# First layer's ffn: the elementwise steps of gate, up half and products dealt out anew over VectorE, ScalarE and GpSimd

## What is computed

```python
def act_qdq(x):
    qmax = 2.0 ** (ACT_BITS - 1) - 1.0
    scale = jnp.maximum(jnp.max(jnp.abs(x)) / qmax, 1e-12)
    return jnp.clip(jnp.round(x / scale), -qmax - 1.0, qmax) * scale

def fixed_qdq_u16(x):
    scale = 1.0 / 65536.0
    return jnp.clip(jnp.round(x / scale), 0.0, 65535.0) * scale
...
x = act_qdq(x)
up = act_qdq(x @ lpbq_dequant(w_up).T)
gate = act_qdq(x @ lpbq_dequant(w_gate).T)
sig = fixed_qdq_u16(jax.nn.sigmoid(gate))
gate = act_qdq(gate * sig)
o = act_qdq(gate * up)
return o @ lpbq_dequant(w_down).T
```

## Time and profile before

| | |
|---|---|
| median of three runs | 1481.43 us (1481.37 to 1482.19) |
| time of the profiled execution | 1482.96 us |
| its span, first to last instruction | 1481.1 us |
| TensorE busy | 1277.1 us (86%) |
| VectorE busy | 848.2 us (57%) |
| ScalarE busy | 697.4 us (47%) |
| GpSimd busy | 269.6 us (18%) |
| mean granted TensorE clock | 0.949 of full speed |

### The profile page before, as it was taken

How to read it: one execution, slowest core, us unless ns; L and a number is a source line. 1 busy time by engine, 2 the same in 40 slices (tenths; PEclk the granted TensorE clock), 3 DMA queues, 4 the chain that set the end, 5 groups by cost and what they waited for, 6 DMA issues and landing times.

```text
span 1481.1 us, 26043 instructions
## 1 busy us (share of the span) xinstructions
PE 1277.1 (86%) x9173; PEld 952.2 (64%) x9173; DVE 848.2 (57%) x1776; ACT 697.4 (47%) x1361; POOL 269.6 (18%) x454
## 2 busy tenths in 40 slices
PE   4799860879988879998888989979999998898989
PEld 2465520446667769876666868668778754456877
DVE  4888679544444456646666443456564466665242
ACT  1566678445533424434444434333433366565453
POOL 1899201000002122331000003042330021100000
PEclk9899975889998979999999999989999999999999
DMA  8000100402220113103404000113101000000000
GB/s 296 1 2 2 47 26 0 191 1 115 101 92 16 51 31 95 56 26 115 182 1 192 1 4 24 43 48 105 42 22 75 1 2 1 1 2 1 1 15 15
DMA packets 42605, 75.69 MB, mean 51 GB/s; under 512 B 3816, under 2 KB 33520, under 8 KB 41584
## 3 DMA queue, kind: packets, MB, share of 16 engines
q1 hardware_dynamic: 38384, 65.62, 12.1%
q0 software_dynamic: 4096, 8.40, 1.9%
HBM read 59.72 MB, written 14.29 MB: 50 GB/s over the span
## 4 chain that ended last, share of the span: by engine, by line
PE 70%; DVE 14%; ACT 8%; issue 5%; POOL 2%; DVEq 1%; DMA 1%; ACTq 0%; SPq 0%; POOLq 0%
PE bank L1576 7%; PE bank L1565 7%; PE bank L1561 6%; PE bank L1620 5%; PE bank L1546 4%; PE bank L1629 4%; PE bank L1547 3%; PE bank L1552 3%; PE bank L1358 3%; PE bank L1424 3%; PE bank L1363 2%; PE bank L1365 2%; PE bank L1364 2%; PE bank L1474 2%; PE bank L1440 1%
## 5 line engine op out<-in xcount | busy, mean ns | idle before, releaser
L1801 ACT ACTIVATE SC<-bank 128x512 f32<-128x512 f32 x192 | 114.3, 596 | 253.6 <-PE bank L1546 133.9
L1888 DVE SCALAR_TENSOR_TENSOR SC<-bank,SM,SC 128x512 f32<-128x512 f32 x128 | 95.9, 749 | 148.0 <-PE bank L1565 108.7
L2458 POOL DMA_INDIRECT xs<-CC,POSI x64 | 62.7, 980 | 564.1 <-DVE POSI L2264 474.6
L1565 PE MATMUL bank<-X,SC 128*128 128x128 f32 x1024 | 140.1, 281 | 14.6 <-DVE SC L2150 14.5
L1576 PE MATMUL bank<-A,SC 128*128 x1024 | 137.0, 277 | 9.0 <-DVE SC L1888 8.3
L1561 PE MATMUL bank<-X,SC 128*128 128x128 f32 x1024 | 140.2, 281 | 5.3 <-ACT SC L1796 5.3
L1561 PEld LDWEIGHTS bank<-X,SC 128*128 128x128 f32 x1024 | 130.9, 198 | 19.5 <-issue 13.6
L1565 PEld LDWEIGHTS bank<-X,SC 128*128 128x128 f32 x1024 | 128.2, 197 | 16.5 <-DVE SC L2150 16.3
L1576 PEld LDWEIGHTS bank<-A,SC 128*128 128x128 f32 x1024 | 126.2, 193 | 18.8 <-issue 18.8
L1620 PE MATMUL bank<-A 128*128 128x128 f32 x736 | 103.5, 286 | 11.5 <-DVE A L2283 10.2
L1712 ACT ACTIVATE A<-bank,SM 128x128 f32<-128x128 f32 x256 | 73.8, 384 | 65.9 <-DVE SM L1984 65.5
(11 more groups left out here) (308 smaller groups left out, 2485.6 us busy)
## 6 DMA issues: line engine op xcount, KB each, us to landing
A<-in_moe SPq DMA_DIRECT2D x36, 768.0 KB, 11.9
A<-xs SPq DMA_DIRECT2D x20, 256.0 KB, 4.3
ys<-A SPq DMA_DIRECT2D x20, 256.0 KB, 2.4
BW<-in_l1f SPq DMA_DIRECT2D x2, 2048.0 KB, 10.4
BW<-in_l2f SPq DMA_DIRECT2D x1, 3456.0 KB, 11.1
BW<-in_l1c SPq DMA_DIRECT2D x1, 3072.0 KB, 16.7
BW<-in_l3f SPq DMA_DIRECT2D x1, 2816.0 KB, 9.6
A<-in_l1c SPq DMA_DIRECT2D x1, 2560.0 KB, 8.5
```

Source lines behind the costliest of these rows:

```text
L1565: m = e.matmul(at["pu"].ap[:, cut(q)], wx[:, cut(4 + q)], x, start=True, stop=True)
L1801: e.activation(at["h"].ap, at["pg"].ap, ACT.Gelu_apprx_tanh).then_inc(at["gelu"][0], 1)
L1888: return e.scalar_tensor_tensor(out=o, in0=a, scalar=s, in1=b, op0=o1, op1=o2)
```

## The change

It deals out steps in another way; the arithmetic of each result stays the same.

- g1 goes from VectorE to GpSimd (`tensor_scalar`) for all twelve items.
- g3 goes from VectorE to ScalarE for the items (0,2) and (1,2), there as two instructions with the constants `P192` and `N192`; the product g4 of these items then cuts off with a minimum.
- `upq` is put into the gate stage's rounds, behind g2 of the same item. For (1,1), (2,1) and (3,1) its first step stays on ScalarE; for the other nine it goes to GpSimd. Its second step is on GpSimd for all twelve. Nothing stands between the reduce and the small steps of the scale any more.
- Products: for m = 0 the second step of p0 and the product go to GpSimd, as a `tensor_scalar` and a `tensor_tensor`; for m = 1 and 2 the product is one `stt` on VectorE.
- `dq`: for m = 0 the second step goes to GpSimd.

Cut to the changed lines and some of what stands around them:

```diff
-        MAG, NMAG = sm(1), sm(1)
+        MAG, NMAG, P192, N192 = sm(1), sm(1), sm(1), sm(1)
...
         def gate_item(n, m):
-            u = {}
+            u, on = {}, "act" if m == 2 and n < 2 else "dve"
...
             def f1():
...
-                at["t"] = u["t"] = tick("f0_vec")
+                at["t"] = u["t"] = tick("f0_ppool")
...
             def f2():
...
+                up_step(n, m)
...
             def f3():
-                at = step("g3", s=u["s"], prev=u["t"])
-                at["t"] = u["t"] = tick("f0_vec")
+                at = step("g3", s=u["s"], prev=u["t"], on=on)
+                if on == "act":
+                    at["grid"] = tick("f0_act")
+                at["t"] = u["t"] = tick("f0_act" if on == "act" else "f0_vec")
...
             def f4():
-                at = step("g4", G=G, s=u["s"], prev=u["t"])
+                at = step("g4", G=G, s=u["s"], prev=u["t"], on=on)
...
         def up_step(n, m):
...
-            at = step("upq", Uq=Uq, ui=ui, us=us, ready=tu_)
-            at["act"], at["t"] = tick("f0_act"), tick("f0_vec")
-            tu[n, m] = at["t"]
+            at = step("upq", Uq=Uq, ui=ui, us=us, ready=tu_, on="act" if m == 1 and n else "pool")
+            at["q"] = tick("f0_act" if at["on"] == "act" else "f0_ppool")
+            at["t"] = tu[n, m] = tick("f0_ppool")
...
         in_order([gate_item(n, m) for n, m in nms], done)
-        g2s, g2i, t2 = scale_of(mg2, 12, sig["g2"], lambda: [up_step(*nm) for nm in nms[:8]])
-        for nm in nms[8:]:
-            up_step(*nm)
+        g2s, g2i, t2 = scale_of(mg2, 12, sig["g2"])
...
         def prod_item(n, m):
-            u = {}
+            u, pooled = {}, m == 0
...
             def f0():
-                at = step("p0", G=G, g2i=g2i, ready=t2)
-                at["q"], at["t"] = tick("f0_act"), tick("f0_act")
-                u["t"] = at["t"]
+                at = step("p0", G=G, g2i=g2i, ready=t2, pooled=pooled)
+                at["q"] = u["t"] = tick("f0_act")
+                if not pooled:
+                    at["t"] = u["t"] = tick("f0_act")
...
             def f1():
-                pooled = m == 1 and n < 3
...
-                at["t"] = u["t"] = tick("f0_vec")
...
-                    at["tp"] = u["t"] = tick("f0_ppool")
+                    at["s"] = tick("f0_ppool")
+                at["t"] = u["t"] = tick("f0_ppool" if pooled else "f0_vec")
...
             def f3():
...
             def s0():
...
-                    at = step("dq", G=gu(n, m)[0], osc=osc, oiv=oiv, on="dve" if m == 2 else "act", ready=t3)
+                    at = step("dq", m=m, G=gu(n, m)[0], osc=osc, oiv=oiv, on="dve" if m == 2 else "act", ready=t3)
...
-                    at["t"] = u[m] = tick("f0_vec")
+                    at["t"] = u[m] = tick("f0_ppool" if m == 0 else "f0_vec")
...
             def s1():
...
                     w.wait_ge(*at["prev"])
...
-                elif kind == "upq":
-                    w.wait_ge(*at["ready"])
-                    e.activation(at["Uq"], at["Uq"], ACT.Identity, scale=at["ui"], bias=MAG).then_inc(at["act"][0], 1)
+                elif kind == "g3" and at["on"] == "act":
+                    w.wait_ge(*at["prev"])
+                    e.activation(at["s"].ap, at["s"].ap, ACT.Identity, bias=P192).then_inc(at["grid"][0], 1)
+                    w.wait_ge(*at["grid"])
+                    e.activation(at["s"].ap, at["s"].ap, ACT.Identity, bias=N192).then_inc(at["t"][0], 1)
+                elif kind == "upq" and at["on"] == "act":
+                    w.wait_ge(*at["ready"])
+                    e.activation(at["Uq"], at["Uq"], ACT.Identity, scale=at["ui"], bias=MAG).then_inc(at["q"][0], 1)
                 elif kind == "p0":
...
                     e.activation(at["G"], at["G"], ACT.Identity, scale=at["g2i"], bias=MAG).then_inc(at["q"][0], 1)
-                    w.wait_ge(*at["q"])
-                    e.activation(at["G"], at["G"], ACT.Identity, bias=NMAG).then_inc(at["t"][0], 1)
+                    if not at["pooled"]:
+                        w.wait_ge(*at["q"])
+                        e.activation(at["G"], at["G"], ACT.Identity, bias=NMAG).then_inc(at["t"][0], 1)
                 elif kind == "dq" and at["on"] == "act":
...
+                    e.memset(P192, 192.0)
+                    e.memset(N192, -192.0)
...
                 elif kind == "f0_ymax":
...
-                elif kind == "g1":
-                    w.wait_ge(*at["prev"])
-                    w.wait_ge(*at["ready"])
-                    ts(at["G"], at["G"], MAGIC, at["gs"], ALU.subtract, ALU.mult).then_inc(at["t"][0], 1)
-                elif kind == "g3":
+                elif kind == "g3" and at["on"] == "dve":
                     w.wait_ge(*at["prev"])
...
                 elif kind == "g4":
                     w.wait_ge(*at["prev"])
-                    stt(at["G"], v4(at["s"].ap), 192.0, at["G"], ALU.subtract, ALU.mult).then_inc(at["t"][0], 1)
+                    if at["on"] == "dve":
+                        stt(at["G"], v4(at["s"].ap), 192.0, at["G"], ALU.subtract, ALU.mult).then_inc(at["t"][0], 1)
+                    else:
+                        stt(at["G"], v4(at["s"].ap), 65535.0 / 65536, at["G"], ALU.min, ALU.mult).then_inc(at["t"][0], 1)
                 elif kind == "g5":
                     w.wait_ge(*at["prev"])
...
-                elif kind == "upq":
-                    w.wait_ge(*at["act"])
-                    w.wait_ge(*at["ready"])
-                    ts(at["Uq"], at["Uq"], MAGIC, at["us"], ALU.subtract, ALU.mult).then_inc(at["t"][0], 1)
-                elif kind == "p1":
+                elif kind == "p1" and not at["pooled"]:
                     w.wait_ge(*at["prev"])
...
-                    if at["pooled"]:
-                        e.tensor_scalar(at["G"], at["G"], at["g2s"], None, ALU.mult).then_inc(at["t"][0], 1)
-                    else:
-                        stt(at["G"], at["G"], at["g2s"], at["Uq"], ALU.mult, ALU.mult).then_inc(at["t"][0], 1)
+                    stt(at["G"], at["G"], at["g2s"], at["Uq"], ALU.mult, ALU.mult).then_inc(at["t"][0], 1)
                 elif kind == "p3":
                     w.wait_ge(*at["prev"])
...
                         ts(at["G"], at["G"], at["oiv"], MAGIC, ALU.mult, ALU.add).then_inc(at["q"][0], 1)
-                    w.wait_ge(*at["q"])
-                    ts(at["G"], at["G"], MAGIC, at["osc"], ALU.subtract, ALU.mult).then_inc(at["t"][0], 1)
+                    if at["m"]:
+                        w.wait_ge(*at["q"])
+                        w.wait_ge(*at["ready"])
+                        ts(at["G"], at["G"], MAGIC, at["osc"], ALU.subtract, ALU.mult).then_inc(at["t"][0], 1)
                 elif kind == "down_x":
...
+                elif kind == "g1":
+                    w.wait_ge(*at["prev"])
+                    w.wait_ge(*at["ready"])
+                    e.tensor_scalar(at["G"], at["G"], -MAGIC, at["gs"], ALU.add, ALU.mult).then_inc(at["t"][0], 1)
+                elif kind == "upq":
+                    w.wait_ge(*at["ready"])
+                    if at["on"] == "pool":
+                        e.tensor_scalar(at["Uq"], at["Uq"], at["ui"], MAGIC, ALU.mult, ALU.add).then_inc(at["q"][0], 1)
+                    w.wait_ge(*at["q"])
+                    e.tensor_scalar(at["Uq"], at["Uq"], -MAGIC, at["us"], ALU.add, ALU.mult).then_inc(at["t"][0], 1)
                 elif kind == "p1" and at["pooled"]:
-                    w.wait_ge(*at["t"])
+                    w.wait_ge(*at["prev"])
...
-                    e.tensor_tensor(at["G"], at["G"], at["Uq"], ALU.mult).then_inc(at["tp"][0], 1)
+                    e.tensor_scalar(at["G"], at["G"], -MAGIC, at["g2s"], ALU.add, ALU.mult).then_inc(at["s"][0], 1)
+                    w.wait_ge(*at["s"])
+                    e.tensor_tensor(at["G"], at["G"], at["Uq"], ALU.mult).then_inc(at["t"][0], 1)
+                elif kind == "dq" and at["m"] == 0:
+                    w.wait_ge(*at["q"])
+                    w.wait_ge(*at["ready"])
+                    e.tensor_scalar(at["G"], at["G"], -MAGIC, at["osc"], ALU.add, ALU.mult).then_inc(at["t"][0], 1)
                 elif kind == "scatter":
```

## The result

| | before | after |
|---|---|---|
| median (lowest to highest) | 1481.40 us (1480.73 to 1482.19, 4 runs) | 1509.68 us (1504.77 to 1511.35, 4 runs) |
| profiled execution, its span | 1482.96, 1481.1 us | 1511.35, 1509.5 us |
| mean granted clock of that span | 0.949 | 0.935 |

The ratio of the times is 1.0185 [1.0161, 1.0209]: slower, as forecast, and by 28.3 us between the medians where 20.2 were forecast. 1509.68 lies outside the range of 1489 to 1507. The profiled execution is the slowest of its four.

The account below looks back on a forecast made before the run. TensorE bounds most of the kernel, but from 209.0 to 261.7 us it idles and the slowest elementwise chain counts. Gate stage 12.7, product stage 1.7 and down input 5.8 give +20.2 on the 1481.43 median: 1501.6 us, range 1489 to 1507.

Parts of the forecast that it names:

- The price of a change: GpSimd switching between maximum over partitions and elementwise work: 6.89 us towards elementwise work, 6.7 towards the maximum, five changes.
- the sign: Whole kernel: slower, chance 0.89; faster 0.05, within 0.2% 0.06.
- the bound: Change towards the maximum: 0 to 6.7 us, from a 6.72 us gap released by VectorE; 6.7 taken.
- Gate stage: Products start at 253.1 instead of 240.40 us, +12.7, behind GpSimd's changes of work and 33 steps.
- 11 products (5.0) and 10 grids (0.5): Gate stage: VectorE's products hold GpSimd up about 0.45 us each, its short grid steps 0.05 each.
- 22.7: Gate stage: GpSimd's 33 steps at 0.66 us plus 9 waits of 0.10, before hold-ups by VectorE.
- its upper bound: Gate stage: each VectorE step holds GpSimd up by its whole length, 0.68 us a product, 0.42 a grid step.
- VectorE's tail: Gate stage, behind the last g1: some 4 us, ending by 248.5, covered by GpSimd's change towards the maximum.
- Product stage and down input: Third maximum starts at T0 + 22.2 against 20.5, +1.7; first down matmul 8.0 behind it against 2.19, +5.8.
- and all that follows move as a block: Down matmuls (13.05 us), next layer's weight load and everything behind shift together, adding nothing to the sum.
- the sum: Gate stage 12.7, product stage 1.7, down input 5.8: +20.2 us for the whole kernel.
- the unknown prices of GpSimd: Range's sources: changes 3 us shorter, about 1489; GpSimd's step 0.1 us dearer and VectorE's waits near upper bound, about 1507.

Follow-up runs that it names:

- the pairs on the second and third chip: Kernel after, unchanged, rerun on two chips of the experiments, against the kernel before there: 1509.42 us against 1484.98, and 1505.97 us against 1484.53.
- the two delays: Kernel before with 37, and with 34, extra absmax on VectorE ahead of the third scale's reduce, GpSimd unchanged: 1506.17 us and 1505.42 us.

## Why the direction was right and the size was not

**The price of a change was right, and decided the sign.** 6.89 was forecast towards elementwise work and 6.99, 6.98 and 7.03 came; 6.7 towards a maximum, and 5.88 and 5.92 came. For the second the bound was taken from a gap that VectorE had ended, so it was too long by 0.8. The Trainium skill's 5.95 us for the load that a first call pays (GPSIMD Engine Reference, section 2.1 Instruction dispatch) fits the changes towards the maximum (5.88 and 5.92) and not those towards elementwise work, which are 1 us longer. The experiment without maxima on GpSimd shows the changes to be the cause: without them the same elementwise work costs 2.1 us in the stage.

**Gate stage: +12.7 forecast, +14.1 came.** The mis-sized term is "11 products (5.0) and 10 grids (0.5)", the time for which VectorE holds GpSimd up: 5.5 us forecast, 7.2 measured. A step alone takes 0.68 to 0.69 (0.67 to 0.68 from start to start, 0.66 forecast), but from 218.34 to 248.67 the 33 steps took 30.3 us, 7.6 over 22.7; 7.2 us is by how much fourteen of them were longer than one alone. Steps of 1.35 to 1.49 lost a whole VectorE product, 0.66 and more, where 0.45 had been taken; the forecast had that as its upper bound. VectorE's grid steps lost too: 573 ns against 419. The longer change (0.1) and the longer steps (2.1) add 2.2 us, the shorter change back gives 0.8 of it back. VectorE's tail lay under that change, as the forecast had it.

**Product stage and down input** came as worked out: +2.0 against +1.7, +6.0 against +5.8. GpSimd's first product step started 6.56 us behind ScalarE's first step (forecast 6.5), and its last product ended at 16.6 (forecast 15.5). The third maximum waited for the change back, not for VectorE, whose reduce ended 1.9 us before.

**The step that failed** is "and all that follows move as a block", a term of nothing in the sum. The stage was 22.1 to 22.8 us longer in every trace of the kernel after; 22.1 is 1.9 us over the sum and would have stayed inside the range. The other 6 of the 8 us by which the median missed are not in the stage: the first trace has down matmuls that are 0.7 us shorter and 6.2 us more behind them. The runs show in place of the zero a term that scatters, from -1.6 to +6.2 us, with the granted clock behind the stage. The kernel before scatters as well: on the third chip its 17 runs beside the experiments go from 1481.28 to 1488.49 us, the longest of them at the lowest mean clock, 0.944. Its four runs beside the first result, 1480.73 to 1482.19, all lie at the low end of that, so that pair shows +28.3 between the medians, and the pairs on the second and third chip +24.4 and +21.4: 6.2 and 2.2 us above the extra of the stage, and 1.3 below it. How far the first median missed is thus in part a matter of the executions, or the chip, that the first pair was taken from. The range allowed for the unknown prices of GpSimd and gave nothing to this term; 2.7 us more at the upper end would have held the result.

What is not settled is why the low stretches fall longer in one execution than in another, and whether a later start of the layers behind makes them longer on average. The kernels with stages 20 to 22 us longer have 1200.0 to 1207.6 us behind them, the others 1198.8 to 1201.7; but the medians of the two delays leave only 0.7 and 0.3 us for it. These are too few to say.

## What to carry to other kernels

Before a step goes to GpSimd, write out the order of its queue in that stage and count where it alternates between a maximum over partitions and elementwise work; each place cost 6 to 7 us here, unless the other engines had that much to do meanwhile. Taking the maxima off GpSimd removed nearly the whole loss and still did not beat the kernel before; what did was to do once, on a scalar, a multiplication that had been done on twelve tiles, and to leave all products to VectorE. And microseconds that turn up behind the edited stage are not explained until the same kernel, and the old kernel with a plain delay, have been run and traced again, more than once.

## What the runs showed of the hardware that was not expected

- The two directions of GpSimd's change differ: 6.80 to 7.47 us towards elementwise work (whose input had been there for 0.6 us or more each time), 5.73 to 6.17 us towards the maximum where no other engine ended the gap. In all nine traces that have it, its MODIFY_POOL_CONFIG stands within 0.3 us of the end of the work in front of it, ahead of the wait of the instruction that it is for.
- Where a VectorE product begins in the first 0.33 us of a GpSimd step of one input in the gate stage, GpSimd's step takes 1.21 to 1.49 us instead of 0.69, and the product keeps its 0.67 to 0.68. Where it began 0.4 us into one (twice), that step kept its 0.69, the product took 0.82 to 0.83, and GpSimd's next step 1.10.
- One kernel's stretch of 1200 us behind the stage differed by 7.6 us between three executions, with 68.3 to 95.6 us of it at the lower clock.
